# One-hots of two tables side by side: tensor_scalar with a column of codes for each chunk, and a ring of three pairs

## The reference

```python
e = stack([tbl_f[ids[:, f]] for f in range(32)], axis=1)   # 2048 x 32 x 64
gram = einsum('bnd,bmd->bnm', e, e)
z = gram[:, rows, cols]                                    # the 496 pairs above the diagonal
h = concatenate([z, dense_ctx], axis=1)                    # 496 + 16 = 512
h = maximum(h @ W_top1 + b_top1, 0)                        # 512 -> 512
h = maximum(h @ W_top2 + b_top2, 0)                        # 512 -> 256
y = h @ W_top3                                             # 256 -> 1
```

## Time and profile before

| | |
|---|---|
| median of 3 runs | 494.22 us (491.78 to 495.32) |
| the profiled execution | 495.87 us, of which the span from first to last instruction is 493.6 us |
| TensorE | 432.1 us busy, 88% of the span, mean granted clock 0.959 |
| POOL | 407.9 us busy, 83% |
| DVE | 302.9 us busy, 61% |
| ACT | 114.2 us busy, 23% |
| chain that ended last | POOL 82%, issue 9%, PE 4%, DMA 2% |

### The profile page before, as it was taken

The page is one execution under the profiler, slowest core; times in us unless marked ns, Lnnn a source line. Parts: engine busy times, 40 slices in busy tenths (PEclk is TensorE's granted clock), DMA queues, the critical chain, the costliest instruction groups (busy, mean ns, idle before and its releaser), DMA issues.

```text
span 493.6 us, 10400 instructions
## 1 busy us (share of the span) xinstructions
PE 432.1 (88%) x4200; PEld 387.7 (79%) x4200; DVE 302.9 (61%) x369; ACT 114.2 (23%) x206; POOL 407.9 (83%) x522
## 2 busy tenths in 40 slices
PE   5298889989799989978999699988999679984987
PEld 5287789989598889877988599777988679874765
DVE  2499969968672698267925586366935847340400
ACT  2244313122012221231123110321113201230322
POOL 7999889999998899999988999889988999884110
PEclk9699999999999999999999899988999979995999
DMA  4534751012311222112311231122211231121010
GB/s 109 144 139 150 215 136 31 16 20 62 87 37 23 47 60 80 21 44 57 86 23 32 54 101 20 23 54 71 62 23 31 51 106 17 23 43 34 7 39 1
DMA packets 21814, 29.32 MB, mean 59 GB/s; under 512 B 9782, under 2 KB 14070, under 8 KB 20640
## 3 DMA queue, kind: packets, MB, share of 16 engines
q1 hardware_dynamic: 12980, 18.96, 11.3%
q0 software_dynamic: 8384, 8.60, 11.2%
q10 hardware_dynamic: 404, 1.09, 0.6%
HBM read 24.35 MB, written 0.07 MB: 49 GB/s over the span
## 4 chain that ended last, share of the span: by engine, by line
POOL 82%; issue 9%; PE 4%; DMA 2%; SPq 1%; DVE 1%; ACT 1%; DVEq 0%
POOL rows L253 59%; POOL pause L260 22%; PE mlp_ps L328 1%; PE gram_ps L316 1%; SPq L192 1%; PE mlp_ps L338 1%; DVE folded L530 1%; DMA rows<-tbl,index 0%; ACT folded L441 0%; PE gram_ps L352 0%; SPq L219 0%; DMA pairs<-dense 0%; DMA pairs<-folded 0%; DMA index<-ids 0%; PE turn_ps L289 0%
## 5 line engine op out<-in xcount | busy, mean ns | idle before, releaser
L253 POOL DMA_INDIRECT rows<-tbl,index x256 | 293.8, 1148 | 44.5 <-issue 42.1
L303 PE MATMUL turn_ps<-split_sb,onehot 125*128 125x192 bf16 x2272 | 213.5, 251 | 22.9 <-DVE split_sb L544 11.7
L303 PEld LDWEIGHTS turn_ps<-split_sb,onehot 125*128 125x128 bf16 x2272 | 193.7, 100 | 33.7 <-DVE split_sb L544 15.5
L495 DVE TENSOR_TENSOR onehot<-place,codes_wide 125x2048 bf16<-125x2048 f16 (+1 forms) x131 | 174.2, 1331 | 7.1 <-DMA place<-ids_scratch 7.1
L260 POOL MEMSET pause<- 128x384 f32 x256 | 111.5, 436 | 0.2
L503 DVE TENSOR_REDUCE rows<-turn_ps 128x128 f32<-128x384 f32 x128 | 71.1, 556 | 54.0 <-PE turn_ps L303 31.1
L530 DVE COPY_PREDICATED folded<-second_sb,gram_ps 128x512 f32<-128x512 int32 x64 | 46.7, 730 | 82.9 <-issue 47.7
L316 PE MATMUL gram_ps<-emb_t 64*128 64x128 f32 x1024 | 76.4, 288 | 3.7 <-DVE folded L530 2.2
L316 PEld LDWEIGHTS gram_ps<-emb_t 64*128 64x128 f32 x1024 | 63.8, 191 | 19.1 <-issue 14.8
L441 ACT COPY folded<-gram_ps 128x512 f32<-128x512 f32 x64 | 37.6, 587 | 150.4 <-PE gram_ps L316 132.3
L328 PE MATMUL mlp_ps<-pairs,w_sb 128*128 128x256 f32 x256 | 58.5, 383 | 1.2 <-DMA pairs<-dense 1.2
(11 more groups left out here) (28 smaller groups left out, 75.7 us busy)
## 6 DMA issues: line engine op xcount, KB each, us to landing
place<-ids_scratch SPq DMA_DIRECT2D x8, 1000.0 KB
rows<-tbl,index POOLq DMA_INDIRECT x256
pairs<-folded SPq DMA_DIRECT2D x122, 32.0 KB
emb_t<-tbl SPq DMA_DIRECT2D x8, 250.0 KB
folded<-tbl SPq DMA_DIRECT2D x5, 312.5 KB
w_sb<-w SPq DMA_DIRECT2D x1, 1024.0 KB
place<-ids_scratch ACTq DMA_DIRECT2D x1, 750.0 KB
rows<-tbl SPq DMA_DIRECT2D x2, 312.5 KB
```

The source lines that it names most:

```text
L253: nc.gpsimd.indirect_dma_start(rows[:, s % 2, slot, t, :], None, tables[f][:, :], bass.IndirectOffsetOnAxis(index[:, s, t, f:f + 1], 0),). ...
L303: last = nc.tensor.matmul(turn_ps[:, u % 2].rearrange("p k b -> p (k b)")[:, t * PARTS * DIM:(t + 1) * PARTS * DIM], onehot[:, u % RING, c ...
L495: nc.vector.tensor_tensor(onehot[:, u % RING, 0:SPAN[u], :], place[:, parity, u, :].unsqueeze(1).to_broadcast([TP, SPAN[u], SUPER]), codes ...
```

## The change

Units of equal span that follow each other are put in pairs (`PAIRS`): (0,1), (2,3), (4,5), (6,7), (8), (9,10), (11,12), (13,14), (15). The one-hots of a pair are made together: for each of the 8 or 10 chunks one `tensor_scalar` compares the row numbers of both units (2 x 256 fp16 values) with one column of fp32 codes, one value a partition, and writes 512 bf16 values. Units 8 and 15 stand alone, with 256 values an instruction. A step has 80 such instructions, 32 + 30 of 512 values and 8 + 10 of 256, in place of 16 `tensor_tensor` of 2048 or 2560 values. The wide copy of the codes and its two COPY instructions go. The ring holds three pairs in place of four units, and all three are made ahead (before batches 5, 6 and 7); the next pair is made when the second unit of the pair three back has been summed.

```diff
+PAIRS = []
+for u in range(UNITS):
+    if PAIRS and len(PAIRS[-1]) == 1 and SPAN[u] == SPAN[u - 1]:
+        PAIRS[-1].append(u)
+    else:
+        PAIRS.append([u])
+PAIR_OF = [j for j, units in enumerate(PAIRS) for _ in units]
-RING = 4
+RING = 3
-READY_MADE = 3
+READY_MADE = RING
...
-        codes_sb = sb("codes_sb", [TP, sum(SPANS)], fp16)
-        codes_wide = sb("codes_wide", [TP, sum(SPANS), SUPER], fp16)
+        codes_sb = sb("codes_sb", [TP, sum(SPANS)], fp32)
-        onehot = sb("onehot", [TP, RING, SPAN_MAX, SUPER], bf16)
+        onehot = sb("onehot", [TP, RING, SPAN_MAX, 2, SUPER], bf16)
...
-                pe.wait_ge(onehot_ready, n + 1)
+                pe.wait_ge(onehot_ready, len(PAIRS) * s + PAIR_OF[u] + 1)
-                            onehot[:, u % RING, c, P * t:P * (t + 1)],
+                            onehot[:, PAIR_OF[u] % RING, c, u - PAIRS[PAIR_OF[u]][0], P * t:P * (t + 1)],
...
-                nc.vector.tensor_tensor(onehot[:, u % RING, 0:SPAN[u], :],
-                                        place[:, parity, u, :].unsqueeze(1).to_broadcast([TP, SPAN[u], SUPER]),
-                                        codes_wide[:, CODE_AT[SPAN[u]]:CODE_AT[SPAN[u]] + SPAN[u], :],
-                                        ALU.is_equal).then_inc(onehot_ready, 1)
+                for c in range(SPAN[u]):
+                    code = CODE_AT[SPAN[u]] + c
+                    last = nc.vector.tensor_scalar(onehot[:, j % RING, c, 0:many, :], place[:, parity, u:u + many, :],
+                                                   codes_sb[:, code:code + 1], None, ALU.is_equal)
+                last.then_inc(onehot_ready, 1)
...
             def follow(s, units, parity):
                 for u in units:
                     add_parts(s, u, parity)
-                    if u + READY_MADE < UNITS:
-                        make_onehot(s, u + READY_MADE, parity)
+                    j = PAIR_OF[u]
+                    if u == PAIRS[j][-1] and j + RING < len(PAIRS):
+                        make_onehots(s, j + RING, parity)
...
-            for span in SPANS:
-                at = slice(CODE_AT[span], CODE_AT[span] + span)
-                nc.vector.tensor_copy(codes_wide[:, at, :], codes_sb[:, at].unsqueeze(2).to_broadcast([TP, span, SUPER])
-                                      ).then_inc(codes_spread, 1)
-            dve.wait_ge(codes_spread, len(SPANS))
```

More of the change, by code:

```diff
@@ L52 @@
 GRAM_UNITS += [[]] * (GRAM_BATCHES - len(GRAM_UNITS))
-READY_MADE = 3
-assert READY_MADE < RING and READY_MADE <= UNITS and not any(GRAM_UNITS[GRAM_BATCHES - READY_MADE + 1:])
+READY_MADE = RING
+assert len(PAIRS) % RING == 0 and not any(GRAM_UNITS[GRAM_BATCHES - READY_MADE:])
 SP_MOVES = 10
@@ L170, in build @@
         codes_loaded = sem("codes_loaded")
-        codes_spread = sem("codes_spread")
         whole_ids_loaded = sem("whole_ids_loaded")
@@ L223, in refill_place @@
             def refill_place(s, parity, of):
-                sp.wait_ge(onehot_ready, FIRST_UNITS + UNITS * (s - 2))
+                sp.wait_ge(onehot_ready, len(PAIRS) * (s - 1))
                 sp.dma_start(place[:, parity], scratch.ap()[bass.ds(of, 1)].to_broadcast([TP, UNITS, SUPER])
@@ L487, in layer3_drain, with make_onehots @@
                                       mlp_ps[0:1, 1, 0, :].rearrange("o (i q t) -> o i q t", i=QUAD, t=TILES)).then_inc(y_ready, 1)
-            def make_onehot(s, u, parity, first=False, loads=None):
+            def make_onehots(s, j, parity, first=False, loads=None):
+                u, many = PAIRS[j][0], len(PAIRS[j])
                 if first:
                     dve.wait_ge(place_first[PIECE_OF[u]], 16)
-                elif u == 0:
+                elif j == 0:
                     dve.wait_ge(place_loaded[parity], 16 * loads)
-                nc.vector.tensor_tensor(onehot[:, u % RING, 0:SPAN[u], :],
-                                        place[:, parity, u, :].unsqueeze(1).to_broadcast([TP, SPAN[u], SUPER]),
-                                        codes_wide[:, CODE_AT[SPAN[u]]:CODE_AT[SPAN[u]] + SPAN[u], :],
-                                        ALU.is_equal).then_inc(onehot_ready, 1)
+                for c in range(SPAN[u]):
[3 more added lines that the diff above has]
+                last.then_inc(onehot_ready, 1)
             def add_parts(s, u, parity, first=False):
@@ L524, in step @@
                         if k >= GRAM_BATCHES - READY_MADE:
-                            make_onehot(s + 2, k - (GRAM_BATCHES - READY_MADE), parity, loads=loads)
+                            make_onehots(s + 2, k - (GRAM_BATCHES - READY_MADE), parity, loads=loads)
                     if mlp and k == LAYER3_BEFORE:
@@ L547, in _ @@
             dve.wait_ge(codes_loaded, 16)
-            for span in SPANS:
-                at = slice(CODE_AT[span], CODE_AT[span] + span)
-                nc.vector.tensor_copy(codes_wide[:, at, :], codes_sb[:, at].unsqueeze(2).to_broadcast([TP, span, SUPER])
-                                      ).then_inc(codes_spread, 1)
-            dve.wait_ge(codes_spread, len(SPANS))
             take_high(0)
             for u in range(UNITS):
[L555 to L558, removed]
+                j = PAIR_OF[u]
+                if u == PAIRS[j][0]:
+                    if j >= RING:
+                        for done in PAIRS[j - RING]:
+                            add_parts(0, done, 0, first=True)
+                    make_onehots(0, j, 0, first=True)
                 if u + 1 < UNITS:
@@ L561, in _ @@
                 low(u)
[L562 to L565, removed]
+            for j in range(len(PAIRS) - RING, len(PAIRS)):
+                for u in PAIRS[j]:
+                    add_parts(0, u, 0, first=True)
+            for j in range(RING):
+                make_onehots(1, j, 1, loads=1)
             dve.wait_ge(second_loaded, 16)
@@ L605 @@
     codes = given("codes", np.concatenate([span * np.arange(TP)[:, None] + np.arange(span) for span in SPANS], axis=1)
-                  .astype(np.float16))
+                  .astype(np.float32))
     out = nc.dram_tensor("out", (BATCH, 1), mybir.dt.float32, kind="ExternalOutput").ap()
```

## The result

The changed kernel takes **538.83 us** (538.51 to 539.37, four runs); the kernel before, on the same chip, 493.0 (490.95 to 495.32). The ratio is 1.0929, with a 95% interval of 1.0873 to 1.0986: 46 us slower, where 17 faster was forecast, and above the range of 464 to 510.

The account below looks back on a forecast made before the run. POOL, its gathers waiting for one-hots, bounds the kernel, TensorE a close second. Both reach the last group at 430 to 431, not 450.9: 20 us, less 3 for irregularities, 17; from 495.9 to 479, as median 477; range 464 to 510.

Parts of the forecast that it names:

- 428 us to the last group: TensorE's own path in the kernel before: ready for the last group at 428 without its waits for gathered rows.
- some 4 more: TensorE's look-ups behind the wait of 397.49: some 4 us regained, two taking 4.70 us where one takes 1.49.
- the mechanism: POOL's gathers wait for DVE's instructions: beside one-source ones 3.0 us a step in place of 6.0, POOL gaining 21 us.
- shut out by a run: Rival, chance 0.13: DVE doesn't let POOL in between short instructions, 11.4 us of waiting a step, 532 us.
- the one-hots' own cost: DVE's one-hots a step: 20.1 us before, 13.1 after, at 0.18 us for 512 values and 0.11 for 256.
- The upper bound, 22.5: DVE's one-hots, us a step at 0.31 us for 512 values and 0.18 for 256; the lower bound was 3.
- 17 when a MEMSET holds DVE up in turn: DVE's runs of one-hots: 13.1 us of a step, 17 with POOL's MEMSETs holding DVE, up to 0.43 us each.
- that COPY of 1314 ns: First COPY at the start: 1314 ns against 1215 for a same-size `tensor_tensor`, a MEMSET ending 0.23 us behind its start.
- DVE elsewhere costs nothing: DVE's sums and runs, 7.4 us, some 9 with MEMSETs, hide under TensorE's seven look-ups with transposes, 12.3 us.
- the cover: TensorE's 12.3 us of look-ups hiding DVE's work; gone at the slower rate, 10.3 us, over 12 with MEMSETs.
- The rival of the slower rate: Chance 0.12: 0.31 us for 512 values, runs of 22.5 us a step, 31 with MEMSETs, TensorE waiting for sums; about 508.
- The 3 us for the 24 instructions ahead of step 0's first sum: Step 0: three pairs' one-hots, 4.3 us, 5.6 with MEMSETs, precede the first sum; TensorE's third look-up waits, 3 us taken.

## Why the prediction was wrong

**What bounded the kernel** was read half rightly: POOL first, yes, but TensorE was a less close second than I thought. With 428 us to the last group and a tail of 43 it would have taken 470 to 475 by itself, and took 458.8. I had counted the waits for rows (19.2 us) and little of what follows them: 13 us more of busy time, at the lower granted clock. The one term I had for that, "some 4 more", is itself wrong by its rows: two look-ups in 4.70 us where two take 2.98 make 1.7.

**The gathers** came out as the mechanism said, and better: 16.2 us of waiting in place of 50.6 (259.4 less 256 x 0.95), a mean of 1013 ns where about 1.05 us was to show it, none shut out by a run: the longest of the 256 took 1.54 us. The timelines of one round, POOL, then the four instructions of DVE beside it:

```profile
214.51 1.07 POOL L258 DMA_INDIRECT rows<-tbl,index  x1 [0.16 <-issue]
215.58 0.47 POOL L265 MEMSET pause<- 128x384 f32 x1
216.21 1.07 POOL L258 DMA_INDIRECT rows<-tbl,index  x1 [0.16 <-issue]
```
```profile
214.42 0.60 DVE L503 TENSOR_SCALAR onehot<-place,codes_sb 125x512 bf16<-125x512 f16 x2
...
214.94 0.76 DVE L503 TENSOR_SCALAR onehot<-place,codes_sb 125x512 bf16<-125x512 f16 x1
...
215.62 0.58 DVE L503 TENSOR_SCALAR onehot<-place,codes_sb 125x512 bf16<-125x512 f16 x1
...
216.12 0.33 DVE L503 TENSOR_SCALAR onehot<-place,codes_sb 125x512 bf16<-125x512 f16 x1
```

POOL is let in at the seams, and its gather loses 0.12 us. The last gather ended at 437.73, not 428; everything ahead was late, and POOL waited 18.7 us for the rows' buffer to come free. But POOL was no longer what mattered.

**The failed step is the one-hots' own cost.** "I take half the time for each value, 0.18 and 0.11, in sum 13.1 us": the time for a value was right (0.26 ns), the fixed part wasn't. I had 0.04 us, from the difference of two long `tensor_tensor`; it is 0.129, and 80 instructions pay it. Free of POOL, 512 values take 0.262 and 256 take 0.196, 19.8 us a step and 20.5 with the ends of the runs. The upper bound, 22.5, held it; the value taken didn't. The Trainium skill (VectorE: DVE Perf Modes, the section on the TRN2 errata) gives 58 cycles and a quarter cycle a value, 0.194 us for 512, which the 0.202 of a constant from start to start agrees with (the section itself calls the row too low for the duration of a single instruction, and that is 0.287 here); of the column's 0.061 it says nothing, so by it the step would have come to about 14 us, an estimate.

**The second half of the same step is "17 when a MEMSET holds DVE up in turn".** The hold was in it, but small, and for MEMSETs only. In the rows above, the second instruction ends at 215.70, 0.12 behind the gather; the third at 216.20, 0.15 behind the MEMSET. Of 463 distances from start to start of 512-value instructions in runs, 254 lie at 0.26, 102 have a gather's end in them and take 0.63 on average, 103 have a MEMSET's and take 0.49 (four have both). That makes 37 and 23 us over the kernel, and the runs some 31 us a step, not 17. I asked what DVE does to POOL with care, and what POOL does to DVE with one row, that COPY of 1314 ns. The Trainium skill (SBUF — State Buffer, § Who interferes with whom) says that a `tensor_scalar` in a two-port mode and GpSimd exclude each other, a `tensor_tensor` only GpSimd's reads; the runs beside MEMSETs agree, 0.262 to 0.500 and 0.335 unchanged. Its "whoever issues first", turned around, was the warning: it holds against DVE as well. Its "for the whole instruction" is more than the rows show: the `tensor_scalar` pays 0.24 to 0.30 us for a MEMSET of 0.417, and of 128 values next to nothing.

**"DVE elsewhere costs nothing"** was built on that sum and fell with it. I had written that above 0.26 us an instruction the cover is gone; the plain distance is 0.262, with POOL's turns 0.39 on average (31 / 80). The rival of the slower rate named this mechanism, sums and TensorE waiting, and priced it at 508: it had the runs right in effect (31 us a step with MEMSETs, some 31 measured), and still counted 4 us for TensorE's waits where those for sums alone are 34.2. The reason given for it, a slow rate per value, was not so. The 3 us for the 24 instructions ahead of step 0's first sum were 16 over the step (the 24 took 10.2 us, and TensorE's clock fell, which I hadn't costed). The 16 us ahead of step 0 I had at nothing: step 0 begins at 71.4 before and at 87.5 after, at 79.5 with the order alone, at 77.0 without POOL's work and at 80.4 with short MEMSETs; so order, instruction and MEMSETs each have a part in it. It is DVE's work on the tables that comes late there: the 15 us more of waiting for `split_sb`.

**How the 46 us divide.** 16.6 without gathers and MEMSETs (with the errors of both runs 12 to 21). By the starts of the steps, 7 of them are lost ahead of step 0 (77.0 against 70.0). The order with `tensor_tensor` cost 7 to 8, but beside POOL's work; no run has the order alone without it, and since the new one-hots cost DVE no more time there than the old ones, what makes the rest of the 16.6 stays open. Some 29 are POOL's gathers and MEMSETs on DVE. What would remain of them if only the gathers held DVE wasn't measured apart: with MEMSETs of 32 the gathers' share of the runs also fell, from 37 to 15 us, and why a gather holds DVE less behind a short MEMSET stays open.

## What to carry to other kernels

Here the engine that was freed from waiting made the other wait. So price a contention in both directions, with the rows of each, before cutting an instruction into short ones on shared memory. Many short instructions cost their fixed part each, which can't be had from the difference of two long ones; where a step is to hide under another engine's work, reckon with the upper end of the bounds, not the middle. And try the pause first: here one number, the length of a MEMSET that does nothing, was worth 28 us.

## What the runs showed of the hardware

- MEMSETs on POOL, which only write, take a `tensor_scalar` or CAST of 512 16-bit values from 0.262 or 0.20 to 0.50 us from start to start, one for one, and a `tensor_tensor` not at all (0.335 both ways). Eight `tensor_scalar` of 128 or 256 values went from 1.35 to 1.50 and from 1.66 to 2.00 us only.
- A `tensor_scalar` with a column of fp32 codes costs 0.061 us more than with a constant, 0.262 against 0.202 at 512 values.
- In the changed kernel DVE and POOL took turns at the seams of instructions, four instructions of DVE to POOL's round of 1.70 us in the stretch shown; a shorter instruction gave back 26 of 40 us only.
- Between instructions of 256 values with a constant, 0.135 us apart, gathers were kept out for whole runs (29 of 256, up to 3.24 us long through two runs of ten) when the MEMSETs had 32 values, and once in 256 when they had 384.
- A gather beside `tensor_scalar` ends 0.12 us late (1.07 for 0.95), beside `tensor_tensor` 0.93 in the rows shown (1.88), and up to 1.3 in the loop (2.25).
- Without waits for gathered rows TensorE did the same matmuls in 419.1 us busy at a granted clock of 0.985, with them in 432.1 at 0.959.
